# Last stage of a two-layer block on one core: where the gated rows are rounded and where later input rows are turned

## The reference

```python
def _L1_cond2_ref(x, id, W, b):
    return jnp.einsum('bsi,bio->bso', x, W[id]) + b[id][:, None, :]

def _L1_ffn_ref(x, w_gate_up, w_down):
    xq = _ste(x, axis=-1)                  # per row: max|x|/127, round, clip
    w1q = _ste(w_gate_up, axis=-1)
    gate_up = jnp.einsum('bsh,oh->bso', xq, w1q)
    gate, up = (gate_up[..., :I], gate_up[..., I:])        # I = 704
    h = jax.nn.silu(gate) * up
    hq = _ste(h, axis=-1)
    w2q = _ste(w_down, axis=-1)
    return jnp.einsum('bsi,oi->bso', hq, w2q)

x = x + _L1_ffn_ref(_L1_cond2_ref(x, itok_B_0_15, L1_cond2_W, L1_cond2_b), L1_ffn_w_gate_up, L1_ffn_w_down)
```

## Time and profile before

| what | value |
|---|---|
| median of 3 runs | 1397.94 us (1395.5 to 1398.98) |
| the profiled execution | 1397.21 us |
| its span in the trace | 1395.4 us |
| TensorE matmuls busy | 1307.0 us (94%) |
| VectorE busy | 930.4 us (67%) |
| ScalarE busy | 518.5 us (37%) |
| GpSimd busy | 567.4 us (41%) |
| the changed stage | from 1275.8 us to the end, 119.6 us |
| TensorE's mean granted clock | 0.978 of 2.4 GHz |

### The profile page before, as it was taken

The page is one execution under the profiler, slowest core; times in us unless marked ns, Lnnn a source line. Parts: engine busy times, 40 slices in busy tenths (PEclk is TensorE's granted clock), DMA queues, the critical chain, the costliest instruction groups (busy, mean ns, idle before and its releaser), DMA issues. The chain is left out here.

```text
span 1395.4 us, 36886 instructions
## 1 busy us (share of the span) xinstructions
PE 1307.0 (94%) x14806; PEld 1055.5 (76%) x14806; DVE 930.4 (67%) x1822; ACT 518.5 (37%) x1202; POOL 567.4 (41%) x624
## 2 busy tenths in 40 slices
PE   4999999999999999999999989999997789997997
PEld 3788888888888888888878868788775567775665
DVE  3888778887888787788786673343423346666886
ACT  3344444444444444444454222222322223222442
POOL 1756655556665566655565222221312111112111
PEclk9999999999999999999999999999998889997998
DMA  6000000000000000000011120000001700001610
GB/s 201 6 13 13 13 13 14 19 25 13 13 13 13 28 13 13 13 16 22 13 43 58 61 62 1 0 1 0 0 0 65 223 23 0 0 0 40 193 50 23
DMA packets 35536, 46.47 MB, mean 33 GB/s; under 512 B 7214, under 2 KB 24840, under 8 KB 35272
## 3 DMA queue, kind: packets, MB, share of 16 engines
q1 hardware_dynamic: 33048, 43.81, 10.4%
q10 hardware_dynamic: 2272, 0.52, 0.2%
q0 software_dynamic: 80, 0.26, 0.1%
HBM read 42.22 MB, written 2.36 MB: 32 GB/s over the span
## 5 line engine op out<-in xcount | busy, mean ns | idle before, releaser
L448 PE MATMUL OE<-w_o,ogT_s 128*128 128x256 f32 x512 | 137.7, 392 | 0.0
L907 POOL TENSOR_TENSOR hs_lo<-work,hs_hi 128x512 fp32r<-128x512 f32 x44 | 57.9, 1317 | 178.4 <-ACT hs_hi L1209 178.4
L250 POOL TENSOR_TENSOR turned<-raw 128x512 f32<-128x512 f32 x62 | 78.8, 1272 | 121.5 <-DVE raw L683 121.5
L708 DVE RECIPROCAL enz<-SC 128x128 f32<-128x128 f32 x128 | 121.1, 947 | 2.0 <-PE SC L396 1.9
L291 POOL TENSOR_TENSOR exz<-ex,enz 128x256 f32<-128x256 f32 x64 | 47.5, 742 | 132.4 <-ACT ex L611 132.4
L339 PE MATMUL PJ<-hs_hi,w_hi 128*128 128x512 f32 x248 | 101.3, 408 | 0.0
L350 PE MATMUL PJ<-w_hi,hs_hi 128*128 128x512 f32 x256 | 100.6, 393 | 0.0
L350 PE MATMUL PJ<-w_lo,hs_hi 128*128 128x512 f32 x256 | 100.1, 391 | 0.0
L350 PE MATMUL PJ<-w_hi,hs_lo 128*128 128x512 f32 x256 | 99.8, 390 | 0.0
L339 PE MATMUL PJ<-hs_lo,w_hi 128*128 128x512 f32 x248 | 97.2, 392 | 0.0
L339 PE MATMUL PJ<-hs_hi,w_lo 128*128 128x512 f32 x248 | 96.9, 391 | 0.0
(11 more groups left out here) (409 smaller groups left out, 3477.5 us busy)
## 6 DMA issues: line engine op xcount, KB each, us to landing
we_ring<-in_we SPq DMA_DIRECT2D x64, 256.0 KB, 3.1
w_raw<-in_w_slices SPq DMA_DIRECT2D x64, 128.0 KB, 2.5
xres<-in_x SPq DMA_DIRECT2D x2, 1024.0 KB, 8.3
turned<-in_w_slices SPq DMA_DIRECT2D x4, 512.0 KB, 4.4
w_o<-in_wo SPq DMA_DIRECT2D x4, 512.0 KB, 5.2
out_rows<-xres SPq DMA_DIRECT2D x16, 128.0 KB, 1.7
w1r<-in_w1i SPq DMA_DIRECT2D x1, 1408.0 KB, 6.5
raw<-in_w SPq DMA_DIRECT2D x2, 682.0 KB
```

Of the source, the lines that this page charges most:

```text
L250: pool.tensor_tensor(to[:, 0, :], x1c[:, :], x2s[:, :], ALU.subtract)
L448: m = pe.matmul(OE[:, SW:SW + D], ogT_s[:, i % 2, h * P:(h + 1) * P], w_o[i // G % 2][:, h, :], start=(h == 0), stop=(h == HQ - 1))
L708: dve.reciprocal(enz[:, cols], SC[:, SW:2 * SW][:, cols]).then_inc(z_rec, 1)
L907: eng.tensor_tensor(hT[1][s, m % 2, :], h[s, m % 2, :], hT[0][s, m % 2, :].bitcast(F32), ALU.subtract).then_inc(second, 1)
```

## The change

TensorE: `turn_x(g + 3)` moves from behind `experts(g + 2)` to right behind `gate_up(g)`. ScalarE: `xT_out(g + 3)` moves accordingly, ahead of `hT_out(g - 1)`. VectorE: `quantise(g)` follows `hidden(g)` in the same iteration, in place of `quantise(g - 1)` ahead of `hidden(g)`. The two waits that keep the halves of XY apart are set to the new order: a turn of y now waits for one more copy of x, and a turn of x for one less copy of y. Nothing is computed otherwise, and no instruction is added.

```diff
@@ turn_x @@
                 if g >= 3:
-                    pe.wait_ge(yT_ev, g - 1)
+                    pe.wait_ge(yT_ev, g - 2)
@@ turn_y @@
                 pe.wait_ge(y_rnd, g + 1)
-                pe.wait_ge(xT_ev, min(max(3, g + 2), G))
+                pe.wait_ge(xT_ev, min(g + 3, G))
@@ TensorE's loop @@
             for g in range(G):
                 gate_up(g)
+                if g + 3 < G:
+                    turn_x(g + 3)
                 if g >= 1:
                     turn_h(g - 1)
                 else:
@@
                 if g + 2 < G:
                     experts(g + 2)
-                if g + 3 < G:
-                    turn_x(g + 3)
                 if g >= 1:
                     down(g - 1)
@@ ScalarE's loop @@
                 gate(g)
+                if g + 3 < G:
+                    xT_out(g + 3)
                 if g >= 1:
                     hT_out(g - 1)
                 if g + 1 < G:
                     yT_out(g + 1)
-                if g + 3 < G:
-                    xT_out(g + 3)
@@ VectorE's loop @@
             for g in range(G):
-                if g >= 1:
-                    quantise(g - 1)
                 hidden(g)
+                quantise(g)
                 if g + 2 < G:
                     front(g + 2)
                 if g >= 1:
                     back(g - 1)
-            quantise(G - 1)
             back(G - 1)
```

## The result

The changed kernel took 1387.21 us (median of 4 runs, 1386.52 to 1388.71) against 1398.46 us for the kernel before (median of 4, 1395.5 to 1399.5): a ratio of 0.9921, 95% interval 0.9906 to 0.9937. That is 11.25 us less, where 9.24 were forecast (1388.7 us). The profiled execution took 1386.52 us.

The account below looks back on a forecast made before the run. The prediction took a ring of waits between TensorE and VectorE to bound the last stage. Savings summing to 9.24 us, off the profiled 1397.21, gave 1388.0, or 1388.7 us for the median; range 1386.3 to 1392.6.

Parts of the forecast that it names:

- The ring through VectorE's order: Last stage: VectorE's late rounding and TensorE's products wait for each other; moving quantise removes TensorE's wait of 0.56 us per period.
- TensorE's period as the sum of its pieces: Last stage: TensorE's six steps from start to start sum to 5.80 us, the new period, against 6.36 with the wait.
- VectorE's sum of 5.58 as the next bound: Last stage: VectorE's work per period from start to start is 5.58 us, 0.22 under TensorE's, so TensorE bounds.
- The copy of x: ScalarE's copy ends 0.90 us after the turn of x starts, hidden by TensorE's 0.98 with 0.08 to spare; cost 0.
- rival A: Wait moves to ScalarE: turn of y waits 0.2 to 0.3 us in iterations 1 to 12; about 1391.7 us; chance 0.15.
- Iteration 0: Stage's first iteration: no turn of h covers the copy, so the turn of y comes 0.90 us behind the turn of x.
- the head: Stage's start: iteration 2's gate and up was to start at 1297.82 against 1297.92, 0.10 us saved.
- the last rows: Stage's end: last rounding 6.04 us behind the last gate and up against 7.58, as back(14) no longer precedes it; 1.54 saved.
- GpSimd's add beside the first gated product: Last stage: the add now lies beside VectorE's first gated product; bounds 0 to 0.74 us per period, taken as 0.
- Rival B: VectorE becomes the bound: add and first gated product exclude each other, period 6.32 us; 1394.9 us; chance 0.06.
- Rival C: Slower: TensorE's granted clock falls in the stage, half clock adding up to 5.8 us per period; chance 0.05.
- The clock at the end: TensorE's last turn of h and down product: half clock narrowly likelier; full clock would give 1.3 us more, 1387.4 us.

Follow-up runs that it names:

- e1: Kernel before with only VectorE's move, quantise(g) right behind hidden(g); TensorE and ScalarE keep the old order; 1387.15 us, ratio to before 0.9926.
- e2: Changed kernel with VectorE's old order (quantise(g-1) ahead of hidden(g)), so only TensorE's and ScalarE's part remains; 1399.36 us, ratio 1.0012.
- e4: Changed kernel without the product of the low parts of the first weights, 6 instead of 12 matmuls in gate_up; 1385.3 us.
- e6: Changed kernel with the turn of x between the turn of h and the turn of y; 1395.97 us, ratio 0.9987.
- e5: Changed kernel with the largest value of the gated rows taken over 352 of 704 columns; 1390.36 us.
- e8: Changed kernel with TensorE's and ScalarE's old order in iteration 0, and VectorE's front(2) ahead of quantise(0); 1387.79 us, ratio 0.9934.
- e3: Changed kernel, but in the last iteration VectorE does back(14) ahead of quantise(15), as the kernel before did; 1389.25 us.
- e7: Changed kernel, but iteration 0 keeps TensorE's and ScalarE's old order (turn of y, experts, turn of x); 1387.0 us, ratio 0.9928.

## Why the prediction was right, and where it was off

- The ring through VectorE's order, and its opening by `quantise` behind `hidden`: shown. e1 has it alone and gains everything, e2 leaves it and gains nothing.
- TensorE's period as the sum of its pieces, 5.80: measured 5.77. The turn of x takes 0.21 behind gate and up where it took 0.27 behind the experts, the turn of h 0.68 for 0.71 (its own 0.66 and the 0.02 of the copy), and the four other steps 0.01 to 0.02 more each.
- VectorE's sum of 5.58 as the next bound: e4's period is 5.58. Its new link, product to reduction, was put at 0.92 and is 0.92 (1323.99 to 1324.91).
- The first gated product starts 2.59 behind gate and up (2.60), and the last rounding 6.04 behind the last gate and up (6.04). VectorE's wait there was forecast at about 0.2. It shows as a gap of 0.09 between the end of the back and the product, 0.17 from start to start.
- The copy of x: 0.90 forecast, 0.90 in e6 and 0.89 in the changed kernel. That the sum is so near is luck: its pieces were 0.47, 0.38 and 0.05, and are 0.41, 0.38 and 0.10. Cover 0.98 forecast, 0.87 measured, because the turns ahead of it got shorter. So the claims that the copy is hidden with 0.08 to spare and that no iteration behind the first waits for it were wrong, by little: the wait is 0.02, where rival A had 0.2 to 0.3. Some 0.1 us less cover would have cost a microsecond.
- Iteration 0 was off: 5.33 instead of 1292.02-1286.87 = 5.15. The turn of y came 1.06 behind the turn of x, not 0.90. In e6, where two waits that are long met (for `w2_second` and `dg_ev`) stand ahead of the turn of x instead of between it and the turn of y, it is 0.90 and the iteration 5.17. The copy starts 0.42 behind its turn and takes 0.38 in both, so the difference lies behind its end. Why it is longer by 0.16 with the two waits in between no run shows.
- The sum for the stage up to the last rounding: 9.24 forecast, 9.41 measured. By terms: the head costs 0.07 where 0.10 was to be saved, iterations 2 to 12 save 6.48 for 6.16, iteration 13 0.60 for 0.60, iteration 14 0.86 for 0.84, the last rows 1.54 for 1.54. The first two errors partly cancel. The rest of the difference to the measured 10.7 in the spans isn't a term of the sum: 0.60 lies ahead of the stage, and 0.69 is the clock, below; both are chance. The medians differ by 11.25; against the median of 19 later runs of the kernel before, 1397.92, it is 10.7.
- GpSimd's add beside the first gated product: the product takes 0.89 there against 0.88 in the earlier trace rows, and 0.87 in e4, where the add lies beside it too. Of the bounds of 0 to 0.74 it is the lower. Rival B is out. The Trainium skill, SBUF — State Buffer, "Who interferes with whom", says that a VectorE instruction with at most one SBUF input, outside the two-port modes, doesn't contend with GpSimd. The trace agrees, within 0.01 us.
- Rival C did not come: of iterations 1 to 12 none is longer than another by over 0.03 us, with ten transposes in a row in each. The Trainium skill, TensorE: Matmul & The Clock Gate, "PE-mode transpose", holds that transposes don't count as busy in the same way and don't bring the higher clock. This case's traces don't bear it out: the granted clock was at its upper level, 2.4 GHz, in all of the 88 us from 1282 to 1370, and at the stage's start it rose between 1279 and 1280, with nothing but transposes on TensorE from 1275.46 to 1280.53, as in the earlier trace rows.

The clock at the end was forecast at half for both last steps, "narrowly". The changed kernel got half of that: the turn of h at full clock, 0.87, the down product at half, 1.46. Which of the two comes is chance, as the last section shows (first rows: timeline of the changed kernel; second: its TensorE by stretch, as length, busy us, instructions, granted clock, DMA share, GB/s):

```profile
1378.02 0.87 PE L2023 MATMUL HT<-ident,hr 128*128 128x128 f32 x6 [1.51 <-DVE hr L2174]
1379.80 1.46 PE L2031 MATMUL DN<-w2qT,hqT 128*128 128x256 bf16 x6 [0.90 <-ACT hqT L2099]
```

```profile
1378.00:1378.50 0.50, 0.48 (x4) 1.00 0.00 0
1378.50:1379.00 0.50, 0.40 (x4) 0.78 0.00 0
1379.00:1379.50 0.50, 0.00 (x0) 0.50 0.00 0
```

## What to carry to other kernels

When two engines wait for each other in every period, add up each engine's pieces from start to start without its waits: the larger sum is the period once the ring is open, and the smaller one tells how far the next step can go. That holds only while every copy between two steps of one engine is covered by its other work: e6's period is 6.43, above both sums. Look for the instruction that stands in a queue behind work it doesn't need, and move only that; a move of work that no one in the ring waits for (here the turn of x) brings nothing and can add a wait. Check moves at both ends of the loop by hand, since the first and last iterations lack the steps that give cover.

## What the runs showed of the hardware that was not expected

The last part of the program, from the last rounding to the end, has three lengths in ten traces: 6.7, 7.2 to 7.3, and 8.0 to 8.1 us (the last column above), as none, one or both of TensorE's last two steps run at half clock. In e1, e5 and e8 both ran at 2.4 GHz, in the kernel before, e3, e4 and e6 both at 1.2; in the changed kernel, e2 and e7 it fell at the end of the first of the two steps or within the second (which took 1.35 us in e7, 1.46 in the other two). Idleness ahead of the last turn of h doesn't sort them. It was 1.51 us in e6 and 1.20 in e4, which ran that step at half, and 1.50 in e1 and e8 and 1.14 in e5, which ran it in full. It was 2.69 in the kernel before and e3, at half, and also 2.69 in e2, at full clock (timeline of e6, then of e1, then of e2):

```profile
1387.09 1.54 PE L2023 MATMUL HT<-ident,hr 128*128 128x128 f32 x6 [1.51 <-DVE hr L2174]
```

```profile
1379.43 0.88 PE L2023 MATMUL HT<-ident,hr 128*128 128x128 f32 x6 [1.50 <-DVE hr L2174]
```

```profile
1394.03 0.87 PE L2023 MATMUL HT<-ident,hr 128*128 128x128 f32 x6 [2.69 <-DVE hr L2174]
```

The forecast had argued from the length of the gap, and that length decides nothing here. Its choice of half clock was therefore a coin's toss, and such a tail has 1.3 us of play in any forecast.

The front's rounding for group 2 stands 0.30 us idle behind its reciprocal in the changed kernel, e1 and e3 to e7, at the same instruction, and 0.04 in other groups. In e8, with another order ahead of it, it doesn't. It doesn't in the kernel before and in e2 either. What it waits for isn't shown. The 0.16 by which iteration 0 is longer with two long-met waits ahead of the turn of y is as open.
